# Attention over 746 tokens: queries and keys in parts of 512 and 234 instead of two parts of 373

## The chip, the cores and the metric

The kernel runs on one core of one Trainium2 chip. The metric is the device time of one execution in microseconds. The engines are named as the profile names them: PE (TensorE; PEld is its weight load), DVE (VectorE), ACT (ScalarE), POOL (GpSimd) and SP (SyncE, which issues most transfers).

## The reference, cut to what matters

The input holds 16 sequences of 750 frames with 23 features. A five-tap layer turns each into 746 tokens of 128 channels, with a batch norm over all of them. Then come an attention block with 8 heads of 16 channels and a feed-forward block in which a router picks one of 8 experts for each token.

```
h = tdnn(x)                                    # (16, 746, 128), relu, batch norm
z = layernorm(h)
q, k, v = heads(z @ Wq.T + bq), heads(z @ Wk.T + bk), heads(z @ Wv.T + bv)
scores = einsum('bhqd,bhkd->bhqk', q, k) / sqrt(16)
h = h + merge(softmax(scores) @ v) @ Wo.T + bo
z = layernorm(h); e = argmax(z @ Wr + br)
h = h + gate * (relu(z @ W1[e] + b1[e]) @ W2[e] + b2[e])
```

The softmax subtracts the maximum of each query over all 746 keys, so each head needs its scores twice: once to find the maxima, and once, transposed, for the exponentials.

## The kernel before, in words

The kernel is software-pipelined over the 16 sequences. A *body* (function `body(i, par)` of every engine) holds one turn of the pipeline, and there are 19 of them (i from -2 to 16). In a body the scores, exponentials and weighted sums of sequence i run, beside the maxima of sequence i and i+1, the layer norm and projections of sequence i+2, and the output projection, second layer norm and router of sequence i-1. Ahead of the bodies stands the five-tap layer, behind them the expert layer over 101 slots of 128 tokens.

A body has 96 steps, two times 48: heads 0 to 3 (g = 0), then heads 4 to 7 (g = 1). Within each half come two passes of 24 steps, one for each half of the queries (373 of 746). A step takes one head j and one tile of 128 keys (kt; the sixth has 106).

- **PE**, per step: a score quad (L1343; four matmuls of 32 weight columns, recorded at L1247 in `quad`) into one of three score banks, and a maximum quad (L1352) of 128 queries against 373 keys into one of three maximum banks. The maximum quads run `LEAD` = 60 steps ahead of the scores. At the steps of `WEIGH_AT` PE also issues `weigh` (L1312: four fp32 matmuls, exponentials against values), and at those of `FILLS` (L300) a smaller task: HTOK, PROJ, MAX1, XNT, Q, K, V, RANK, MAX0. All tasks of a steady body go through one bank (`misc`), so a task waits (`bank_free`) until the one before it has been read out.
- **ACT**, per step: the exponential of one score bank (L808), into a ring of three groups of four heads in SBUF (`probs`). At `OUT_AT` it copies the finished sum out (L817), and at `EMPTY_AT` it empties the tasks' bank.
- **DVE**, per step: the maximum over one maximum bank (L1112, `half_max`). Between these stand, each at the step that a table gives, the joining of the halves (`maxima`, L935 to L943), transposes and normalisation of the attention output (`T_AT`, `INV_AT`, `MULT_AT`, `BACK_AT`), the residual (`REST_AT`, L988 and L990, which empties PROJ), the layer-norm statistics (`LN1_AT`, `LN2_AT`), the router (`ROUTE_AT`) and the places of the tokens among the experts (`RANK_AT`, L1029 to L1046; its first instruction waits for the task RANK).
- **POOL** finishes the layer norms, splits q and k into bf16 parts and scatters rows; **SP** moves the q and k parts at the steps of `LOAD0_AT` and `LOAD1_AT`.

Every engine walks its own steps in order. What binds them are the rings: PE may write score bank s only when the exponential of step s-3 is done (L1342), and maximum bank m only when the reduction m-3 is done (L1351). So PE can be at most three steps ahead of ACT and of DVE, and a task's step number against the step at which another engine serves it says who has to wait.

Some numbers of the tables, before: RANK is issued at step 77 and DVE takes it up at 78; PROJ at 17 and 27, taken up at 24 and 38; MAX1 at 41, emptied at 42; MAX0 at 88.

Of the kernel before, what the change touches and what calls it, by code (L numbers as in the profile page):

```python
# [5 lines left out]
def audio_tower(  # L6
# [62 lines left out]
    STEPS = H * 2 * NT  # L69
    PASS = NT * GH  # L70
    GROUPS = STEPS // GH
    LEAD = 60


    PARTS = 1
    WEIGH_AT = (7, 11, 15, 19, 23, 27)
    OUT_AT = 4
    LN1_AT = (19, 21, 24, 25, 26, 28)
    LN2_AT = (40, 43, 45, 46, 48, 49)
    GATE_AT, H_AT = 73, (19, 26)  # L80
    T_AT, INV_AT, MULT_AT, BACK_AT, REST_AT = (55, 59, 6, 8), (66, 9), (85, 11), (12, 16), (24, 38)
    ROUTE_AT = (56, 57, 58, 60, 61, 63)
    RANK_AT = (78, 81, 82, 87, 89)
    LOAD1_AT = (26, 29, 32, 35, 38, 40, 46, 48, 50, 52, 54, 56)
    LOAD0_AT = (92, 94, 97, 99, 102, 104, 107, 109, 111, 114, 116, 118)
    SCATTER_AT = (0, 3, 6, 9, 12, 15)
# [12 lines left out]
    with ctx:  # L99
# [8 lines left out]
        RING, QW = N_P * GH * HALF, H * LP // 2  # L108
# [3 lines left out]
        probs = p_ring.rearrange("p (n j t) -> p n j t", n=N_P, j=GH)  # L112
        q_rows = [arena[0:KM, RING + QW * n:RING + QW * (n + 1)].bitcast(bf16).rearrange("p (h t) -> p h t", h=H)
# [15 lines left out]
        half_max = sb("half_max", [128, STEPS])  # L129
        neg_max = sb("neg_max", [128, STEPS // 2])  # L130
# [9 lines left out]
        mv2 = sb("mv2", [128, NT, 2])  # L140
        var_eps2 = sb("var_eps2", [128, NT])
        rstd2 = sb("rstd2", [128, NT])
        by_tok = sb("by_tok", [128, 2, LP])
        r_den = sb("r_den", [128, 2, LP // QUAD])
# [10 lines left out]
        place = sb("place", [128, NT, E])  # L155
        place1 = sb("place1", [128, NT, E])
# [4 lines left out]
        tok_w_sb = sb("tok_w_sb", [TAPS, D])  # L161
# [4 lines left out]
        bo_bc, br_bc, bv_sb = sb("bo_bc", [128, D]), sb("br_bc", [128, E]), sb("bv_sb", [128, 1])  # L166
        wo_wr = sb("wo_wr", [128, D + E])
        wr_c = sb("wr_c", [128, E])
        mean_w = sb("mean_w", [128, 128])
# [4 lines left out]
        bn_stats = sb("bn_stats", [128, 2 * B, 6])  # L174
# [30 lines left out]
        early_e, early_r, early_r0 = sb("early_e", [128, 1]), sb("early_r", [128, 1]), sb("early_r0", [128, 1])  # L205
        slot_e, slot_r, slot_r0 = sb("slot_e", [128, 1]), sb("slot_r", [128, 1]), sb("slot_r0", [128, 1])
        slot_e_i, slot_r_i = sb("slot_e_i", [1, 128], i32), sb("slot_r_i", [1, 128], i32)

        def of_ring(first, n):
# [93 lines left out]
        EMPTY_AT = {("HTOK", 0): 9, ("HTOK", 1): 14, ("MAX1", 0): 42, ("XNT", 0): 46, ("XNT", 1): 50,  # L303
                    ("Q", 0): (53, 54), ("Q", 1): (57, 58), ("K", 0): (61, 62), ("K", 1): (66, 70),
                    ("V", 0): 73, ("V", 1): 86, ("MAX0", 0): 88}
# [134 lines left out]
        def step_of(s):  # L440
            p, kt, j = s // PASS, s % PASS // GH, s % GH
            return p // 2, p % 2, kt, GH * (p // 2) + j, j
# [17 lines left out]
        def _(sp):  # L460
# [56 lines left out]
            def body(i, par):  # L517
# [27 lines left out]
                if live(i, 2):  # L545
                    if not is_body(i, FIRST_BODY):
                        store_q(i, (1, 2))
                        store_k(i, 1)
                        store_k(i, 2)
                    if live(i, 0):  # L550
                        sp.wait_ge(s_st, scores(i, STEPS // 2 - 1))
                    load_first_heads(i, par)
# [177 lines left out]
        def _(act):  # L730
# [67 lines left out]
            def body(i, par):  # L798
                if is_body(i, FIRST_BODY + 1):
                    constants()  # L800
                for s in range(STEPS):
                    if live(i, 0):
                        g, qh, kt, h, j = step_of(s)
                        G = s // GH
                        if j == 0:
                            wait(act, s_pv, i * GROUPS + (G - N_P + 1))
                        act.wait_ge(s_st, scores(i, s))
                        nc.scalar.activation(probs[0:kn(kt), G % N_P, j, :], st_bank[s % N_ST][0:kn(kt), 0:HALF],  # L808
                                             ACT.Exp).then_inc(s_exp, 1)
                    if s % PASS == OUT_AT:  # L810

                        b, p = (i, s // PASS - 1) if s >= PASS else (i - 1, 3)
                        if live(i, 0 if s >= PASS else -1):
# [3 lines left out]
                            nc.scalar.copy(o_un[:, p // 2, p % 2 * HALF:(p % 2 + 1) * HALF], o_bank[:, 0:HALF])\  # L817
                              .then_inc(s_o, 1)
# [54 lines left out]
        def _(dve):  # L873
# [55 lines left out]
            def maxima(b, g, n):  # L929

                k = 3 * g
                full = neg_max[:, 24 * g:24 * (g + 1)].rearrange("p (h t) -> p t h", h=GH)
                if n == 0:
                    dve.wait_ge(s_red, b * STEPS + STEPS // 2 * (g + 1))
                    nc.vector.tensor_reduce(neg_max[:, 24 * g:24 * (g + 1)],  # L935
                                            half_max[:, 48 * g:48 * (g + 1)].rearrange("p (n a) -> p n a", a=2),
                                            AX.X, ALU.max, negate=True).then_inc(s_max, 1)
                elif n == 1:
                    dve.wait_ge(s_max, b * 6 + (k + 1))
                    nc.vector.tensor_copy(max_parts[:, g, :, 0, :], full).then_inc(s_max, 1)  # L940
# [158 lines left out]
            def body(i, par):  # L1099
# [4 lines left out]
                for s in range(STEPS):  # L1104
# [5 lines left out]
                    if 0 <= b < B:  # L1110
                        dve.wait_ge(s_mx, b * STEPS + (m + 1))
                        nc.vector.tensor_reduce(half_max[:, m:m + 1], mx_bank[m % N_MX][:, 0:HALF], AX.X, ALU.max)\  # L1112
                          .then_inc(s_red, 1)
                    for g, at in ((1, STEPS - 1 - LEAD), (0, STEPS + STEPS // 2 - 1 - LEAD)):
# [20 lines left out]
                    if s == 33 and is_body(i, FIRST_BODY):  # L1135
# [11 lines left out]
                    if s == 72 and is_body(i, LAST_BODY):  # L1147
# [3 lines left out]
                    if s == 60 and is_body(i, FIRST_BODY):  # L1151
# [69 lines left out]
        def _(pe):  # L1221
# [77 lines left out]

            def weigh(b, G, k):  # L1300

                p, kt = G // NT, G % NT
                first = HALF * k // PARTS
                n = HALF * (k + 1) // PARTS - first
                if k == 0:
                    pe.wait_ge(s_exp, scores(b, GH * (G + 1) - 1))
                    if kt == 0:
                        wait(pe, s_o, b * 4 + p)  # L1310
                for j in range(GH):
                    last = nc.tensor.matmul(o_bank[32 * j:32 * (j + 1), first:first + n],  # L1312
                                            values[b % 3][0:kn(kt), kt, GH * (p // 2) + j, :],
                                            probs[0:kn(kt), G % N_P, j, first:first + n],
                                            start=kt == 0 and k == 0, stop=kt == NT - 1, skip_group_check=True)
                if k == PARTS - 1:
                    last.then_inc(s_pv, 1)
# [12 lines left out]
            def body(i, par):  # L1330
# [6 lines left out]
                for s in range(STEPS):  # L1337
                    if live(i, 0):
                        g, qh, kt, h, j = step_of(s)
                        if s % 48 == 0:  # L1340
                            pe.wait_ge(s_mrow, i * 64 + 32 * (g + 1))
                        wait(pe, s_exp, scores(i, s) - N_ST)  # L1342
                        quad(st_bank[s % N_ST][0:kn(kt), 0:HALF], k_rows[par][0:KM, h, D * kt:D * kt + kn(kt)],  # L1343
                             q_rows[par][0:KM, h, qh * HALF:(qh + 1) * HALF]).then_inc(s_st, 1)
                    b, m = maximum_of(i, s)
                    if 0 <= b < B:

                        h, t, half = m // 12, m % 12 // 2, m % 2
                        if m % 48 == 0:
                            pe.wait_ge(s_ld[m // 48], b * 192 + 192)  # L1350
                        wait(pe, s_red, b * STEPS + (m + 1 - N_MX))  # L1351
                        quad(mx_bank[m % N_MX][:, 0:HALF], q_rows[b % 2][0:KR, h, D * t:D * (t + 1)],  # L1352
                             k_rows[b % 2][0:KR, h, half * HALF:(half + 1) * HALF]).then_inc(s_mx, 1)
                    for n, after in enumerate(WEIGH_AT):

                        p = (s - after) // PASS
                        if (s - after) % PASS == 0 and live(i, 0 if p >= 0 else -1):
                            weigh(i if p >= 0 else i - 1, p % 4 * NT + n // PARTS, n % PARTS)
                    if is_body(i, LAST_BODY) and s == WEIGH_AT[-1] - PASS + 1:
# [87 lines left out]
```

## Time and profile before

| | |
|---|---|
| time, median of 3 runs | 1233.38 us (1231.71 to 1234.83) |
| span of the profiled execution | 1275.9 us |
| PE busy | 1178.7 us, 92% of the span |
| DVE busy | 1072.5 us, 84% |
| ACT busy | 950.6 us, 75% |
| POOL busy | 680.0 us, 53% |
| chain that ended last, by engine | PE 63%, DVE 20%, issue 5%, POOL 3%, ACT 2% |
| L1112, DVE reductions of 373 | 1536, 760.8 us busy, mean 534 ns |
| L808, ACT exponentials of 373 | 1536, 655.0 us busy, mean 489 ns |
| L1247, score and maximum quads | 2 x 6144 matmuls of 373 columns, 515.7 and 519.1 us busy |
| L1312, weighing, fp32 | 3072 records, 313.2 us busy |

The profile gives no time of the profiled execution besides its span. That span is 42.5 us above the median of the timed runs. Matmuls overlap, so the durations of a line of PE are longer than what each adds; the distance from one start to the next is the better measure, and the same holds for DVE and ACT when they run back to back.

### The profile page before, as it was taken

The numbers are of one execution on the slowest core, as the hardware profiler recorded it, in microseconds if no ns is written. First come the engines' busy times: TensorE is split into PE (matmuls) and PEld (weight loads), VectorE is DVE, ScalarE is ACT, GpSimd is POOL, SyncE is SP. The second block draws the span as 40 slices with busy tenths as digits, with TensorE's granted clock in tenths as the row PEclk, the third lists the DMA queues.
The fourth block names the chain that finished last, engine by engine and source line by source line (L and its number), as shares of the span: only waits on it lengthen the run. The fifth ranks groups of instructions, "written<-read, shape, count | busy, mean of one in ns | idle before, by whom it ended". The sixth has DMA issues, their size and how long they took to land.

```text
span 1275.9 us, 53879 instructions
## 1 busy us (share of the span) xinstructions
PE 1178.7 (92%) x21379; PEld 745.5 (58%) x21379; DVE 1072.5 (84%) x2756; ACT 950.6 (75%) x2477; POOL 680.0 (53%) x894
## 2 busy tenths in 40 slices
PE   6479999999999999999999999999999846899996
PEld 3334656555555556555555556565644326899996
DVE  7469899999999999999999999999999544577774
ACT  4426988888887878788888878797877824567774
POOL 2062436566473837475665739374723334456664
PEclk9768999999999999999999999999999969899998
DMA  8152132222313131323223131313220513333331
GB/s 190 39 84 79 40 86 72 76 84 61 94 52 94 45 105 42 104 72 79 83 63 93 51 94 45 106 41 104 72 80 28 150 56 105 88 93 105 103 101 50
DMA packets 79409, 102.32 MB, mean 80 GB/s; under 512 B 15916, under 2 KB 72995, under 8 KB 78734
## 3 DMA queue, kind: packets, MB, share of 16 engines
q1 hardware_dynamic: 70624, 79.02, 23.4%
q0 software_dynamic: 8384, 20.22, 5.1%
q8 instruction: 158, 2.59, 0.9%
q14 instruction: 57, 0.47, 0.1%
q10 hardware_dynamic: 186, 0.02, 0.0%
HBM read 60.76 MB, written 38.93 MB: 78 GB/s over the span
## 4 chain that ended last, share of the span: by engine, by line
PE 63%; DVE 20%; issue 5%; POOL 3%; ACT 2%; DMA 1%; SPq 1%; another core or an unknown queue 1%; POOLq 0%; DVEq 0%; ACTq 0%
PE psum L1247 36%; DVE half_max L1112 14%; PE psum L1312 13%; PE psum L1391 6%; PE psum L1401 5%; PE psum L1252 2%; ACT arena L808 2%; DVE stats L916 1%; POOL out_dram L720 1%; DVE rows L990 1%; PE psum L1382 1%; POOL arena L405 1%; DMA arena<-max_rows 1%; PE psum L1267 1%; DVE arena L962 1%
## 5 line engine op out<-in xcount | busy, mean ns | idle before, releaser
L1112 DVE TENSOR_REDUCE half_max<-psum 128x1 f32<-128x373 f32 x1536 | 760.8, 534 | 62.8 <-PE psum L1247 55.0
L808 ACT ACTIVATE arena<-psum 128x373 f32<-128x373 f32 (+1 forms) x1536 | 655.0, 489 | 154.4 <-PE psum L1247 139.0
L1247 PE MATMUL psum<-k_rows,arena 96*32 96x373 bf16 x6144 | 519.1, 329 | 14.9 <-DVE half_max L1112 6.1
L1247 PE MATMUL psum<-arena,k_rows 98*32 98x373 bf16 x6144 | 515.7, 326 | 13.7 <-ACT arena L808 6.2
L1312 PE MATMUL psum<-arena,values 128*32 128x373 f32 (+1 forms) x3072 | 313.2, 478 | 0.2
L1247 PEld LDWEIGHTS psum<-k_rows,arena 96*32 96x32 bf16 x6144 | 173.8, 96 | 195.7 <-DVE half_max L1112 103.4
L1247 PEld LDWEIGHTS psum<-arena,k_rows 98*32 98x32 bf16 x6144 | 176.4, 95 | 178.2 <-ACT arena L808 74.8
L631 POOL DMA_INDIRECT routed_rows_dram<-rows,pos_i x96 | 96.6, 1007 | 170.7 <-PE psum L1247 106.2
L720 POOL DMA_INDIRECT out_dram<-arena,slot_id x101 | 119.2, 1180 | 90.0 <-issue 51.5
L1312 PEld LDWEIGHTS psum<-arena,values 128*32 128x32 f32 (+1 forms) x3072 | 98.4, 110 | 20.7 <-issue 2.8
L861 ACT COPY arena<-psum 128x128 f32<-128x128 f32 x101 | 26.9, 266 | 77.7 <-PE psum L1382 39.7
L639 POOL TENSOR_TENSOR m_diff<-stats 128x6 f32<-128x6 f32 x15 | 3.1, 203 | 147.1 <-DVE stats L916 147.1
L1391 PE MATMUL psum<-arena,seq 128*128 128x128 f32 x544 | 75.3, 283 | 5.1 <-issue 2.4
L852 ACT ACTIVATE arena<-psum,seq 128x128 f32<-128x128 f32 x272 | 77.8, 370 | 0.5 <-issue 0.5
L1401 PE MATMUL psum<-seq,arena 128*128 128x128 f32 x544 | 73.8, 280 | 0.3 <-ACT arena L852 0.3
L1391 PEld LDWEIGHTS psum<-arena,seq 128*128 128x128 f32 x544 | 69.1, 199 | 6.5 <-issue 5.0
L405 POOL TENSOR_SCALAR arena<-h_cur,m_mean,rstd 128x128 f32<-128x128 f32 x90 | 70.9, 800 | 3.3 <-POOL rstd L665 3.3
L405 POOL TENSOR_SCALAR rows<-rows,n_mean,rstd 128x128 f32<-128x128 f32 x90 | 70.8, 796 | 0.0
L1401 PEld LDWEIGHTS psum<-seq,arena 128*128 128x128 f32 x544 | 67.6, 195 | 0.5 <-ACT arena L852 0.5
L1097 DVE COPY seq<-seq 128x1156 f32 x68 | 53.6, 788 | 11.1 <-issue 1.4
L950 DVE STREAM_TRANSPOSE by_tok<-o_un 128x384 f32<-128x384 f32 x64 | 36.2, 566 | 18.7 <-ACT o_un L817 18.7
L1209 DVE TENSOR_TENSOR arena<-psum,seq 128x128 f32<-128x128 f32 x68 | 19.8, 291 | 35.3 <-PE psum L1401 30.9
(218 smaller groups left out, 1447.5 us busy)
## 6 DMA issues: line engine op xcount, KB each, us to landing
arena<-q_parts_dram SPq DMA_DIRECT2D x192, 93.2 KB, 2.4
k_rows<-k_parts_dram SPq DMA_DIRECT2D x192, 93.2 KB, 2.4
arena<-routed_rows_dram SPq DMA_DIRECT2D x101, 130.0 KB
q_parts_dram<-q_part SPq DMA_DIRECT2D x48, 186.5 KB, 2.3
k_parts_dram<-k_part SPq DMA_DIRECT2D x48, 186.5 KB, 2.0
arena<-in_x_t_dram SPq DMA_DIRECT2D x3, 703.1 KB, 14.1
seq<-in_w_dram SPq DMA_DIRECT2D x1, 2048.0 KB
seq<-in_w_dram SPq DMA_DIRECT2D x8, 256.0 KB
```

What stands on the lines that cost most here:

```text
L405: last = ops.tensor_scalar(dst(t), src(t), mean_var[:, t, 0:1], r_root[:, t:t + 1], ALU.subtract, ALU.mult)
L631: pool.indirect_dma_start(out=rows_dram, out_offset=bass.IndirectOffsetOnAxis(ap=pos_i[:, t:t + 1], axis=0), in_=rows[:, t, :], in_offset= ...
L720: pool.indirect_dma_start(out=out_rows, out_offset=bass.IndirectOffsetOnAxis(ap=slot_id[:, n:n + 1], axis=0), in_=slot_y[n][:, :], in_offs ...
L808: nc.scalar.activation(probs[0:kn(kt), G % N_P, j, :], st_bank[s % N_ST][0:kn(kt), 0:HALF], ACT.Exp).then_inc(s_exp, 1)
L852: last = nc.scalar.activation(slot_ht[n % 2][:, D * k:D * (k + 1)], psum[:, 2 + n % 2, D * k:D * (k + 1)], ACT.Relu, bias=slot_w[n % N_W][ ...
L950: nc.vector.transpose(by_tok[:, g, first:first + LP // 2], o_un[:, g, first:first + LP // 2])\
L1097: nc.vector.tensor_copy(slot_w[n % N_W].unsqueeze(1), w_sb[:, bass.ds(e, 1), :]).then_inc(s_fw, 1)
L1112: nc.vector.tensor_reduce(half_max[:, m:m + 1], mx_bank[m % N_MX][:, 0:HALF], AX.X, ALU.max)\
L1247: last = nc.tensor.matmul(dst[n:n + m], weights[:, n:n + m], moving, start=start, stop=stop)
L1312: last = nc.tensor.matmul(o_bank[32 * j:32 * (j + 1), first:first + n], values[b % 3][0:kn(kt), kt, GH * (p // 2) + j, :], probs[0:kn(kt), ...
L1391: last = nc.tensor.matmul(psum[:, 2 + n % 2, D * k:D * (k + 1)], slot_w[n % N_W][:, W1 + D * k:W1 + D * (k + 1)], slot_xt[n % 2][:, :], st ...
L1401: last = nc.tensor.matmul(psum[:, 5 + n % 3, 0:D], slot_ht[n % 2][:, D * k:D * (k + 1)], slot_w[n % N_W][:, W2 + D * k:W2 + D * (k + 1)], ...
```

## The change: what it does

Each head's 746 queries (for the scores) and 746 keys (for the maxima) are cut at 512. The 512 fill one PSUM bank alone (a *wide* step); the 234 of two heads share one bank (a *narrow* step, 468 columns, two quads on PE, one instruction on ACT or DVE). A body then has 72 steps, two halves of 36. For the scores, 24 wide steps come first in each half, then 12 narrow ones. For the maxima, each run of three steps is wide, wide, narrow.

- PE issues as many quads as before (96 of 512 columns and 96 of 234 in place of 192 of 373). `weigh` runs in 6 wide and 6 narrow groups a half, at new steps.
- The ring of exponentials is larger (three groups of 4 x 512), and the narrow exponentials use the same memory in six pieces, so ACT waits on other `weigh` groups (`weighed_before`).
- The output copy is of 512 and then of 234 columns; `turn` waits for the copy that its half needs.
- All step tables are rewritten for 72 steps. RANK is now issued at step 61, and DVE takes it up at step 58. PROJ is issued at 13 and 21 and taken up at 18 and 28. MAX1 is issued at 29. V's second part comes after RANK and MAX0. `LEAD` is 48.
- Some small tiles share memory with others (`place` with `scored`, `mv2` with `mv`, tables and constants in `by_tok`).

```
-    STEPS = H * 2 * NT
-    LEAD = 60
-    WEIGH_AT = (7, 11, 15, 19, 23, 27)
-    OUT_AT = 4
-    LN1_AT = (19, 21, 24, 25, 26, 28)
-    T_AT, INV_AT, MULT_AT, BACK_AT, REST_AT = (55, 59, 6, 8), (66, 9), (85, 11), (12, 16), (24, 38)
-    RANK_AT = (78, 81, 82, 87, 89)
+    WIDE_Q = 512
+    NARROW_Q = L - WIDE_Q
+    WIDE_STEPS = NT * GH
+    HALF_STEPS = WIDE_STEPS + NT * GH // 2
+    STEPS = 2 * HALF_STEPS
+    LEAD = 48
+    WEIGH_AT = (7, 11, 15, 19, 23, 27, 31, 32, 34, 35, 37, 39)
+    OUT_AT = (28, 40)
+    LN1_AT = (14, 15, 17, 18, 19, 21)
+    T_AT, INV_AT, MULT_AT, BACK_AT, REST_AT = (41, 44, 5, 6), (50, 7), (64, 8), (9, 12), (18, 28)
+    RANK_AT = (58, 60, 61, 65, 67)
...
-        FILLS = (("HTOK", 0, 9), ("HTOK", 1, 13), ("PROJ", 0, 17), ("PROJ", 1, 27), ("MAX1", 0, 41), ("XNT", 0, 46),
-                 ("XNT", 1, 49), ("Q", 0, 53), ("Q", 1, 57), ("K", 0, 61), ("K", 1, 65), ("V", 0, 73),
-                 ("RANK", 0, 77), ("V", 1, 85), ("MAX0", 0, 88))
+        FILLS = (("HTOK", 0, 5), ("HTOK", 1, 9), ("PROJ", 0, 13), ("PROJ", 1, 21), ("MAX1", 0, 29), ("XNT", 0, 33),
+                 ("XNT", 1, 36), ("Q", 0, 41), ("Q", 1, 45), ("K", 0, 49), ("K", 1, 53), ("V", 0, 57),
+                 ("RANK", 0, 61), ("MAX0", 0, 65), ("V", 1, 69))
...
+                        if wide:
+                            nc.scalar.activation(probs[0:kn(kt), kt % N_P, j, :], st_bank[s % N_ST][0:kn(kt), 0:WIDE_Q],
+                                                 ACT.Exp).then_inc(s_exp, 1)
+                        else:
+                            nc.scalar.activation(narrow_probs[0:kn(kt), kt, NARROW_Q * j:NARROW_Q * (j + 2)],
+                                                 st_bank[s % N_ST][0:kn(kt), 0:2 * NARROW_Q],
+                                                 ACT.Exp).then_inc(s_exp, 1)
...
+                        n, part = m // 3, m % 3
+                        if part < 2:
+                            nc.vector.tensor_reduce(half_max[:, n, part:part + 1], mx_bank[m % N_MX][:, 0:WIDE_Q], AX.X, ALU.max)\
+                              .then_inc(s_red, 1)
+                        else:
+                            nc.vector.tensor_reduce(half_max[:, n, 2:4],
+                                                    mx_bank[m % N_MX][:, 0:2 * NARROW_Q].rearrange("p (a t) -> p a t", a=2),
+                                                    AX.X, ALU.max).then_inc(s_red, 1)
...
+                            for n in range(2):
+                                last = quad(st_bank[s % N_ST][0:kn(kt), NARROW_Q * n:NARROW_Q * (n + 1)],
+                                            k_rows[par][0:KM, h + n, D * kt:D * kt + kn(kt)], q_rows[par][0:KM, h + n, WIDE_Q:L])
+                            last.then_inc(s_st, 1)
```

## Rows read from the trace of the kernel before

**Rows 1.** The page: the span, and the engines' busy time

```profile
span 1275.9 us, 53879 instructions
...
PE 1178.7 (92%) x21379; PEld 745.5 (58%) x21379; DVE 1072.5 (84%) x2756; ACT 950.6 (75%) x2477; POOL 680.0 (53%) x894
```

**Rows 2.** Stretches: one steady body, then RANK's end to MAX1, MAX1 to RANK's end

```profile
core 0: us, PE busy (x) PEld busy (x) DVE busy (x) ACT busy (x) POOL busy (x), PEclk, DMA share, GB/s
561.08:619.65 58.57, 57.76 (x1228) 33.21 (x1224) 54.85 (x140) 49.24 (x123) 35.91 (x51) 1.00 0.28 76
558.18:594.24 36.06, 35.25 (x752) 18.85 (x737) 34.04 (x88) 28.73 (x73) 16.02 (x22) 1.00 0.34 91
594.24:616.76 22.52, 22.52 (x493) 14.34 (x493) 20.82 (x53) 20.53 (x51) 19.90 (x30) 1.00 0.18 51
```

**Rows 3.** Timeline of DVE: the joining of the maxima (start us, us, engine, line)

```profile
210.56 0.20 DVE L935 TENSOR_REDUCE neg_max<-half_max 128x24 f32<-128x48 f32 x1
...
913.84 0.20 DVE L935 TENSOR_REDUCE neg_max<-half_max 128x24 f32<-128x48 f32 x1
```

**Rows 4.** The chain that ended last, in order of time: start us, us, what

```profile
561.53 0.35 DVE place L1039
...
563.67 0.47 DVE arena L962
...
587.29 0.20 DVE stats L916
...
588.59 3.17 DVE half_max L1112 x7
...
591.79 0.20 DVE neg_max L935
...
592.44 0.18 DVE max_parts L940
...
593.07 0.10 DVE max_parts L943
...
593.63 0.09 DVE raw L988
593.72 0.47 DVE rows L990
...
594.24 0.39 PE psum L1267 x4
...
957.33 0.48 DVE by_tok L950
```

**Rows 5.** Timeline of PE and PEld: weighing, score and maximum quads, RANK

```profile
600.15 0.11 PEld L1247 LDWEIGHTS psum<-k_rows,arena 96*32 96x32 bf16 x4
...
610.69 0.83 PE L1312 MATMUL psum<-arena,values 128*32 128x373 f32 x8
611.32 0.37 PE L1247 MATMUL psum<-arena,k_rows 98*32 98x373 bf16 x4
611.48 0.37 PE L1247 MATMUL psum<-k_rows,arena 96*32 96x373 bf16 x4
...
616.51 0.20 PE L1247 MATMUL psum<-onehot,before 128*32 128x56 bf16 x4
616.54 0.30 PE L1247 MATMUL psum<-onehot,ones_b 128*32 128x48 bf16 x24
616.70 0.24 PE L1247 MATMUL psum<-zero_b,ones_b 128*32 128x56 bf16 x4
616.76 0.35 PE L1247 MATMUL psum<-arena,k_rows 98*32 98x373 bf16 x4
```

**Rows 6.** Timeline of DVE: a reduction of 48 elements and the next start

```profile
955.53 0.20 DVE L1002 TENSOR_REDUCE top<-logits 128x6 f32<-128x48 f32 x1 [0.46 <-POOL logits L695]
955.65 0.54 DVE L1112 TENSOR_REDUCE half_max<-psum 128x1 f32<-128x373 f32 x1
```

**Rows 7.** Timeline of ACT: exponentials back to back, after the last maximum

```profile
1012.70 1.60 ACT L808 ACTIVATE arena<-psum 128x373 f32<-128x373 f32 x4 [0.18 <-PE psum L1247]
...
1014.48 1.60 ACT L808 ACTIVATE arena<-psum 106x373 f32<-106x373 f32 x4 [0.18 <-PE psum L1247]
```

More of the change, by code:

```diff
@@ L154, in audio_tower @@
         g_inv = sb("g_inv", [128, NT])
-        place = sb("place", [128, NT, E])
-        place1 = sb("place1", [128, NT, E])
+        place, place1 = scored, scored2
         pos = sb("pos", [128, NT])
@@ L204, in audio_tower @@
         late_base, late_first = sb("late_base", [128, 1]), sb("late_first", [128, 1])
-        early_e, early_r, early_r0 = sb("early_e", [128, 1]), sb("early_r", [128, 1]), sb("early_r0", [128, 1])
-        slot_e, slot_r, slot_r0 = sb("slot_e", [128, 1]), sb("slot_r", [128, 1]), sb("slot_r0", [128, 1])
-        slot_e_i, slot_r_i = sb("slot_e_i", [1, 128], i32), sb("slot_r_i", [1, 128], i32)
+        slot_cols = sb("slot_cols", [128, 6])
+        early_e, early_r, early_r0, slot_e, slot_r, slot_r0 = (slot_cols[:, n:n + 1] for n in range(6))
+        slot_e_i, slot_r_i = (by_tok[0:1, 0, D * n:D * (n + 1)].bitcast(i32) for n in range(2))
         def of_ring(first, n):
@@ L440, in step_of, with last_step_of, weighed_before @@
         def step_of(s):
-            p, kt, j = s // PASS, s % PASS // GH, s % GH
-            return p // 2, p % 2, kt, GH * (p // 2) + j, j
+            g, r = s // HALF_STEPS, s % HALF_STEPS
+            if r < WIDE_STEPS:
+                return g, True, r // GH, r % GH
+            return g, False, (r - WIDE_STEPS) // 2, (r - WIDE_STEPS) % 2 * 2
+        def last_step_of(G):
+            g, n = G // HALF_GROUPS, G % HALF_GROUPS
+            return HALF_STEPS * g + (GH * n + GH - 1 if n < NT else WIDE_STEPS + 2 * (n - NT) + 1)
+        def weighed_before(i, g, wide, kt):
+            first = i * GROUPS + g * HALF_GROUPS
+            if not wide:
+                return first + NT // 2 + kt // 2 + 1
+            return first + kt - 2 if kt >= N_P else first - NT + 2 * kt + 2
         def load_patches(engine, c, low, high):
@@ L550, in body @@
                     if live(i, 0):
-                        sp.wait_ge(s_st, scores(i, STEPS // 2 - 1))
+                        sp.wait_ge(s_st, scores(i, HALF_STEPS - 1))
                     load_first_heads(i, par)
@@ L802, in body @@
                     if live(i, 0):
-                        g, qh, kt, h, j = step_of(s)
-                        G = s // GH
+                        g, wide, kt, j = step_of(s)
                         if j == 0:
-                            wait(act, s_pv, i * GROUPS + (G - N_P + 1))
+                            wait(act, s_pv, weighed_before(i, g, wide, kt))
                         act.wait_ge(s_st, scores(i, s))
[L808 to L813, printed above, removed]
+                        if wide:
[5 more added lines that the diff above has]
+                                                 ACT.Exp).then_inc(s_exp, 1)
+                    for p, at in ((0, OUT_AT[0]), (1, OUT_AT[1]), (2, HALF_STEPS + OUT_AT[0]), (3, OUT_AT[1] - HALF_STEPS)):
+                        b, ahead = (i, 0) if p < 3 else (i - 1, -1)
+                        if s == at and live(i, ahead):
                             act.wait_ge(s_pv, b * GROUPS + NT * (p + 1))
@@ L931, in maxima @@
                 k = 3 * g
-                full = neg_max[:, 24 * g:24 * (g + 1)].rearrange("p (h t) -> p t h", h=GH)
+                n_g = GH * NT
+                full = neg_max[:, n_g * g:n_g * (g + 1)].rearrange("p (u t a) -> p t u a", u=2, a=2)
+                high, low = (max_parts[:, g, :, part, :].rearrange("p t (u a) -> p t u a", a=2) for part in range(2))
                 if n == 0:
-                    dve.wait_ge(s_red, b * STEPS + STEPS // 2 * (g + 1))
-                    nc.vector.tensor_reduce(neg_max[:, 24 * g:24 * (g + 1)],
-                                            half_max[:, 48 * g:48 * (g + 1)].rearrange("p (n a) -> p n a", a=2),
+                    dve.wait_ge(s_red, b * STEPS + HALF_STEPS * (g + 1))
+                    nc.vector.tensor_reduce(neg_max[:, n_g * g:n_g * (g + 1)].rearrange("p (n a) -> p n a", a=2),
+                                            half_max[:, n_g // 2 * g:n_g // 2 * (g + 1), :].rearrange("p n (c a) -> p n a c", c=2),
                                             AX.X, ALU.max, negate=True).then_inc(s_max, 1)
@@ L1134, in body @@
                             layer_moments(stats, mv, var_eps, s_ln, 0)
-                    if s == 33 and is_body(i, FIRST_BODY):
+                    if s == 24 and is_body(i, FIRST_BODY):
                         dve.wait_ge(s_ln_p, 1)
@@ L1146, in body @@
                             layer_moments(stats2, mv2, var_eps2, s_ln2, B - 1)
-                    if s == 72 and is_body(i, LAST_BODY):
+                    if s == 54 and is_body(i, LAST_BODY):
                         dve.wait_ge(s_ln2_p, ln2_p_done(B - 1) + 3)
@@ L1150, in body @@
                                   mv2, rstd2, s_ln2_p)
-                    if s == 60 and is_body(i, FIRST_BODY):
+                    if s == 55 and is_body(i, FIRST_BODY):
                         split(dve, nc.vector, s_apart_v, i, "Q")
@@ L1298, in task, with weigh @@
                 last.then_inc(s_misc, 1)
[L1300 to L1310, printed above, removed]
-                for j in range(GH):
[L1312 to L1317, printed above, removed]
+            def weigh(b, G):
+                g, n = G // HALF_GROUPS, G % HALF_GROUPS
+                wide, kt = n < NT, n % NT
+                pe.wait_ge(s_exp, scores(b, last_step_of(G)))
+                if kt == 0:
+                    wait(pe, s_o, b * 4 + G // NT)
+                for j in range(GH):
+                    if wide:
+                        moving = probs[0:kn(kt), kt % N_P, j, :]
+                    else:
+                        moving = narrow_probs[0:kn(kt), kt, NARROW_Q * j:NARROW_Q * (j + 1)]
+                    last = nc.tensor.matmul(o_bank[32 * j:32 * (j + 1), 0:WIDE_Q if wide else NARROW_Q],
+                                            values[b % 3][0:kn(kt), kt, GH * g + j, :], moving,
+                                            start=kt == 0, stop=kt == NT - 1, skip_group_check=True)
+                last.then_inc(s_pv, 1)
             def constants():
@@ L1345, in body @@
                     b, m = maximum_of(i, s)
                     if 0 <= b < B:
-                        h, t, half = m // 12, m % 12 // 2, m % 2
-                        if m % 48 == 0:
-                            pe.wait_ge(s_ld[m // 48], b * 192 + 192)
+                        u, t, n = m // (3 * NT), m % (3 * NT) // 3, m % 3
+                        if m % HALF_STEPS == 0:
+                            pe.wait_ge(s_ld[m // HALF_STEPS], b * 192 + 192)
                         wait(pe, s_red, b * STEPS + (m + 1 - N_MX))
-                        quad(mx_bank[m % N_MX][:, 0:HALF], q_rows[b % 2][0:KR, h, D * t:D * (t + 1)],
-                             k_rows[b % 2][0:KR, h, half * HALF:(half + 1) * HALF]).then_inc(s_mx, 1)
@@ L1354, in body @@
-                    for n, after in enumerate(WEIGH_AT):
[L1356 to L1359, printed above, removed]
+                        if n < 2:
+                            quad(mx_bank[m % N_MX][:, 0:WIDE_Q], q_rows[b % 2][0:KR, 2 * u + n, D * t:D * (t + 1)],
+                                 k_rows[b % 2][0:KR, 2 * u + n, 0:WIDE_Q]).then_inc(s_mx, 1)
+                        else:
+                            for a in range(2):
+                                last = quad(mx_bank[m % N_MX][:, NARROW_Q * a:NARROW_Q * (a + 1)],
+                                            q_rows[b % 2][0:KR, 2 * u + a, D * t:D * (t + 1)],
+                                            k_rows[b % 2][0:KR, 2 * u + a, WIDE_Q:L])
+                            last.then_inc(s_mx, 1)
@@ L1360, in body @@
+                    for n, after in enumerate(WEIGH_AT):
+                        for g in (0, 1):
+                            at = HALF_STEPS * g + after
+                            if at % STEPS == s and live(i, -(at // STEPS)):
+                                weigh(i - at // STEPS, HALF_GROUPS * g + n)
+                    if is_body(i, LAST_BODY) and s == WEIGH_AT[-1] - HALF_STEPS + 1:
                         pe.wait_ge(s_early, EARLIES)
```

65 lines of the change are left out of this document (32 added, 33 removed).

## The prediction

> **What bounds the kernel now.** I read the page first: PE is busy for 92% of the span and DVE for 84% [rows 1], so neither is plainly the bound. Next come the stretches of one steady body. The joining of the first maxima comes back twelve times between 210.56 and 913.84 us [rows 3], 58.6 us apart on average, and the body cut out for closer reading takes 58.57 us at a granted clock of 1.00 [rows 2]. Sixteen such bodies make some 940 of the 1275.9 us. Last, the chain in order of time shows that the bound changes inside a body. From MAX1 to RANK the chain is PE's alone, and PE is busy for 22.52 of 22.52 us [rows 2]. From RANK round to the next MAX1, 36.06 us, the chain jumps between runs of DVE reductions (seven in 3.17 us), the small DVE work between them, and PE [rows 4]. I call the first the PE stretch and the second the DVE stretch.
>
> The DVE stretch by counts: DVE passes steps 78 to 95 and 0 to 38, 57 reductions of 3.17 / 7 = 0.453 us [rows 4], 25.8 us. Between them stand, by [rows 4], two joinings of maxima (0.20 + 0.18 + 0.10 each, 0.96), two normalisations (0.47 each, 0.94), four transposes (0.48 each, 1.92), six statistics (0.20, 1.2), two residuals (0.09 + 0.47, 1.1), the ranks (0.35 and four small ones at 0.12 [rows 6], 0.8) and a reciprocal (0.2): 7.1. Together 32.9, so 3.2 of the 36.06 us are neither: DVE waited for a bank that PE had not yet filled, or for a semaphore.
>
> PE in the same stretch: 60 steps of two quads at 0.160 us (611.32 to 611.48) make 19.2, and 15 weighings at 0.63 (610.69 to 611.32) 9.5 [rows 5]: 28.7 plus tasks. In the PE stretch it is 36 steps (11.5) and 9 weighings (5.7), 17.2, so tasks and rests take 22.52 - 17.2 = 5.3. The tasks of the DVE stretch are of the same kind and I put them at no more than that.
>
> **The change part by part.**
>
> *PE's work: nothing.* A score or maximum quad takes 0.160 us at 373 columns. Six quads of RANK, 28 columns on average, take 0.16 together (616.54 to 616.70), 0.027 each [rows 5]. The line between them gives 0.214 at 512 and 0.106 at 234. A pair costs 0.320 either way, and there are 96 pairs before and after. Weighing in proportion to columns: 0.865 wide and 0.395 narrow, the sum of two unchanged. Bounds for a narrow quad: 0.100 (pure proportion) to 0.160 (no cheaper than now, if its weight loads, 0.11 us for four [rows 5], came to the surface). I take 0.106, since RANK's quads load just as many weights and pass at 0.027.
>
> *DVE's reductions: 1.7 us less a body.* A reduction of 48 elements lets the next start after 0.12 us [rows 6], one of 373 after 0.453: 1.025 ns an element. That makes 0.595 at 512 and 0.550 at 468, 0.580 on average. 96 x 0.453 = 43.5 becomes 48 x 0.595 + 24 x 0.550 = 41.8. Bounds: 0 (pure proportion) to 2.9 (24 instructions at the 0.12 of the shortest). In the DVE stretch alone it is 42 x 0.580 = 24.4 for 25.8, 1.4 less.
>
> The Trainium skill, "VectorE: DVE Perf Modes", section on the TRN2 errata, gives an operation that reads PSUM a fixed 120 cycles, 125 ns at 0.96 GHz, beside one cycle an element. By it a reduction of 373 would take 0.513, and the DVE stretch would lose about 2.3 us in place of 1.4 (an estimate from that page), some 14 us over sixteen bodies. The trace has 0.453 from start to start, so I stay with the row.
>
> *ACT's exponentials: nothing on the path.* Four in a row take 1.60 us, and in the tail the next four start 1.78 us after the first [rows 7]. The columns of a body are the same (96 x 373), so ACT's work at worst stays as it is, and at best it falls by as much per instruction as DVE's does. ACT is busy for 49.24 of 58.57 us [rows 2] and keeps that slack.
>
> *The rings in time: longer.* Three banks are still three steps, but a step lasts 58.57 / 72 = 0.81 us for 0.61, so that DVE's small work of 0.2 to 0.5 us is covered better. This is the gain that I can't count, only bound: between none and all of the 3.2 us.
>
> *Two meetings: new waits.* RANK goes out on PE at step 61, and DVE takes it up at 58, where before it was 77 and 78. DVE must stand at step 58, with reductions 59, 60 and 61 queued behind it, until PE has done steps 59 to 61 and the task. PE can do that much (maximum 61 needs reduction 58 alone), so there is no deadlock, but PE then stands before maximum 62 until DVE has taken up RANK and done reduction 59. At the other end MAX1 (PE step 29) needs the bank that DVE empties at the end of its step 28; before it was 41 against 38. So PE may not be three steps ahead there, but must wait for DVE. Between the meetings nothing can be carried over from one stretch into the other: a body is the DVE chain from RANK to MAX1, and then PE's work from MAX1 to RANK.
>
> What the trace of before shows of such a stand: `top` sat 0.46 us for POOL, and the reduction behind it started 0.12 us after it, not before [rows 6]. The Trainium skill says so too ("PSUM — Partial Sum Buffer", Engine vs sequencer instructions: the queue of VectorE is strict FIFO). If the reductions could pass, the stand would cost DVE nothing, about 0.4 us a body less, and 1220 in place of the forecast; by this rule they can't.
>
> *The sum of a body.* DVE stretch: DVE now passes steps 59 to 71 and 0 to 28, 42 reductions, 24.4, and the same 7.1: 31.5. PE there: 40 steps of two quads at 0.213 (17.0), 7 wide and 6 narrow weighings (6.1 + 2.4), 25.5, plus at most 5.3: 30.8. So DVE sets it. To this I add 1.0 us for rests: 0.4 at the meeting (from RANK's last quad to reduction 59), and about 0.1 a step in steps 71 to 4, where no small work stands on DVE (five reductions 2.9) and PE needs as long (five steps 2.1 and two narrow weighings 0.8). Before those, DVE starts three full banks behind, and from step 5 on it carries transposes, normalisation and statistics, so it can't run dry. 32.5. PE stretch: 22.52, with 32 steps (13.6) and 5 wide and 6 narrow weighings (4.3 + 2.4) in place of 17.2: 25.6. Together 58.1 for 58.57, 0.5 us less, 8 us over sixteen bodies.
>
> *Both ends.* `LEAD` is two thirds of a body where it was five eighths: before the first scores DVE needs 48 x 0.580 = 27.8 for 60 x 0.453 = 27.2, 0.6 more. After the last maximum the same share of scores runs alone, with a fifth fewer exponentials; I take nothing for it, bounds -2 to +1. Shared tiles, later loads and the fewer steps of SP and POOL I put at nothing: POOL is busy for 35.91 of 58.57 us [rows 2]. If that cover were gone, a wait of DVE for POOL like the 0.46 of [rows 6] would come once a body, 7 us.
>
> In all 7.4 us less: 1268.5 for the span of 1275.9. The span is 42.5 us above the median of the timed runs, and I know no reason why the bodies should be what differs, so I take the same 7.4 from 1233.4: 1226.
>
> **The rivals.**
>
> - *The meetings eat more than the longer rings give: slower.* Place: DVE's stand at step 58 and PE's at MAX1. If the DVE stretch keeps all of its 3.2 us of rests, the body is 31.5 + 3.2 + 25.6 = 60.3, 28 us slower in all, 1261; half way, 1245. It decides as soon as the rests exceed 58.57 - 57.1 = 1.5 us. For it: those 3.2 us came about with a freer coupling than the new one. Against it: the reductions behind the stand have their banks full. 25%.
> - *No rests at all:* DVE is never short between the meetings, 31.5 + 25.6 = 57.1 or a little less, 24 to 28 us gained, 1207. For it: longer rings. Against it: every semaphore hop. 12%.
> - *It comes out even:* rests of 1.3 to 1.7, 1230 to 1237. 17%.
> - *The change doesn't do what it says, because narrow quads are no cheaper:* 96 x (0.160 - 0.106) = 5.2 us a body, 1316. RANK's row speaks against it. 3%.
>
> **How the numbers follow.** A measurement of this kernel can tell about 0.3%, 3.7 us, from no change. The forecast (rests 0.4 to 1.3; 1217 to 1230) holds 43%, and with the case of no rests faster gets 55%. Even gets 17%, and the two slower cases 28%. The range leaves out the lower half of the no-rests case, the upper part of the slower rival and the last: 1206 to 1252.
>
> **What would show it.** In the profile after, reductions of 512 and 468 should start 0.595 and 0.550 apart, narrow quads 0.106. The body should be 58.1 us. DVE should have one idle piece before `place` (L1029 before), released by PE's RANK, of 0.5 to 2 us in every body, and PE an idle piece before MAX1, released by DVE's `rows`. From MAX1 to RANK PE should be busy throughout for 25.6 us. The prediction is wrong if a narrow quad costs more than 0.12, if the DVE stretch is above 33.5 us, or if another wait (POOL's logits, a q or k load) shows up once a body.

## The result and the profile after

The changed kernel takes 1247.06 us (median of 4 runs, 1246.54 to 1248.33) against 1233.55 for the kernel before. The ratio is 1.0105, with a 95% interval of 1.009 to 1.0121: 13.5 us slower, where 7.4 us faster was forecast.

A span of a steady body is best taken from the joining of the maxima. These are the first and the last of thirteen such rows, twelve bodies apart, from DVE's timeline of the changed kernel (start us, us, engine, line).

```profile
206.79 0.20 DVE L957 TENSOR_REDUCE neg_max<-half_max 128x24 f32<-128x48 f32 x1
...
904.77 0.20 DVE L957 TENSOR_REDUCE neg_max<-half_max 128x24 f32<-128x48 f32 x1
```

That is 58.17 us a body (twelve bodies in 697.98 us), where 58.1 was forecast. The page's span, and the stretches of the prediction, in the changed kernel: one body, RANK's end to MAX1, MAX1 to RANK's end (columns as in [rows 2]).

```profile
span 1244.7 us, 53111 instructions
```

```profile
core 0: us, PE busy (x) PEld busy (x) DVE busy (x) ACT busy (x) POOL busy (x), PEclk, DMA share, GB/s
556.06:614.17 58.11, 55.78 (x1224) 32.97 (x1224) 53.35 (x115) 47.89 (x97) 35.98 (x51) 1.00 0.27 76
555.02:587.37 32.35, 30.35 (x693) 17.64 (x679) 31.75 (x71) 25.52 (x52) 13.98 (x21) 1.00 0.35 99
587.37:613.10 25.73, 25.40 (x547) 15.29 (x548) 21.61 (x45) 22.33 (x47) 21.97 (x31) 1.00 0.16 47
```

The two stretches are 32.35 and 25.73 us; forecast were 32.5 and 25.6. Against [rows 2] the first is 3.7 shorter, the second 3.2 longer. By the two profiles the change should have made the kernel faster, and indeed its span, 1244.7, is 31 us below the 1275.9 of [rows 1]. But the timed runs of the kernel before take 1233.5. So the profile of before may not be typical, and the first experiment takes it again.

### The profile page after: what moved, and what is told of

Same layout as the page of the kernel before. It is cut to its first block, busy times and chain, and to the rows that moved or that the text cites. A ratio compares the mean times of both kernels' runs of the same rounds, so it can differ in the third digit from the quotient of the medians.

```text
span 1244.7 us, 53111 instructions
## 1 busy us (share of the span) xinstructions
PE 1138.9 (92%) x21379; PEld 741.4 (60%) x21379; DVE 1048.7 (84%) x2372; ACT 926.6 (74%) x2093; POOL 679.9 (55%) x894
## 4 chain that ended last, share of the span: by engine, by line
PE 56%; DVE 23%; POOL 10%; issue 4%; ACT 1%; DMA 1%; SPq 1%; POOLq 0%; DVEq 0%; ACTq 0%
PE psum L1274 28%; PE psum L1339 11%; DVE half_max L1135 11%; PE psum L1431 7%; PE psum L1441 7%; POOL arena L407 6%; DVE half_max L1138 5%; DVE stats L936 2%; POOL rstd L682 2%; PE psum L1279 1%; DVE by_tok L971 1%; DVE merged_t L992 1%; PE psum L1422 1%; DVE arena L983 1%; ACT arena L825 1%
## 5 line engine op out<-in xcount | busy, mean ns | idle before, releaser
L1135 DVE TENSOR_REDUCE half_max<-psum 128x1 f32<-128x512 f32 x768 | 508.1, 678 | 35.3 <-PE psum L1274 32.7
L1274 PE MATMUL psum<-k_rows,arena 96*32 96x512 bf16 (+1 forms) x6144 | 462.0, 326 | 24.4 <-DVE half_max L1138 10.5
L825 ACT ACTIVATE arena<-psum 128x512 f32<-128x512 f32 (+1 forms) x768 | 428.2, 600 | 66.5 <-PE psum L1274 60.2
L1274 PE MATMUL psum<-arena,k_rows 98*32 98x512 bf16 (+1 forms) x6144 | 458.2, 322 | 2.8 <-ACT arena L825 1.4
L1339 PE MATMUL psum<-arena,values 128*32 128x234 f32 (+3 forms) x3072 | 313.9, 476 | 0.8 <-ACT arena L828 0.4
L1138 DVE TENSOR_REDUCE half_max<-psum 128x2 f32<-128x468 f32 x384 | 243.1, 633 | 8.3 <-PE psum L1274 7.0
L828 ACT ACTIVATE arena<-psum 128x468 f32<-128x468 f32 (+1 forms) x384 | 198.0, 557 | 66.3 <-PE psum L1274 64.0
```

Source lines behind the costliest of these rows:

```text
L825: nc.scalar.activation(probs[0:kn(kt), kt % N_P, j, :], st_bank[s % N_ST][0:kn(kt), 0:WIDE_Q], ACT.Exp).then_inc(s_exp, 1)
L828: nc.scalar.activation(narrow_probs[0:kn(kt), kt, NARROW_Q * j:NARROW_Q * (j + 2)], st_bank[s % N_ST][0:kn(kt), 0:2 * NARROW_Q], ACT.Exp). ...
L1135: nc.vector.tensor_reduce(half_max[:, n, part:part + 1], mx_bank[m % N_MX][:, 0:WIDE_Q], AX.X, ALU.max)\
L1138: nc.vector.tensor_reduce(half_max[:, n, 2:4], mx_bank[m % N_MX][:, 0:2 * NARROW_Q].rearrange("p (a t) -> p a t", a=2), AX.X, ALU.max).the ...
L1274: last = nc.tensor.matmul(dst[n:n + m], weights[:, n:n + m], moving, start=start, stop=stop)
L1339: last = nc.tensor.matmul(o_bank[32 * j:32 * (j + 1), 0:WIDE_Q if wide else NARROW_Q], values[b % 3][0:kn(kt), kt, GH * g + j, :], moving, ...
```

## The experiments

### The kernel before, profiled once more (e1)

No edit.

> The kernel before, unchanged, profiled once more. The profile that the prediction was read from has a span of 1275.9 us, 42 above the timed median, while the changed kernel's profile (1244.7) agrees with its timed runs. Theory A (that profile was of an untypical execution, and its steady body of 58.57 us was too long): the span is now 1230 to 1236 and the steady body 56 to 57 us, so that the changed kernel's 58.1 is 1 to 2 us a body worse. Theory B (the bodies were typical and only front and tail were stretched): the span is 1230 to 1236 but the steady body is again 58.5 us and the 42 us lie ahead of the first and behind the last joining of maxima (97.6 and 277 us in that profile; 94.3 and 259.5 in the changed kernel's). Then the changed kernel would lose in front and tail, not in the bodies.

The span is now 1232.6 us, in line with the timed runs. From the page, DVE's timeline (again first and last of thirteen) and the stretches of this run of the kernel before:

```profile
span 1232.6 us, 53879 instructions
```

```profile
209.42 0.20 DVE L935 TENSOR_REDUCE neg_max<-half_max 128x24 f32<-128x48 f32 x1
...
889.80 0.20 DVE L935 TENSOR_REDUCE neg_max<-half_max 128x24 f32<-128x48 f32 x1
```

```profile
core 0: us, PE busy (x) PEld busy (x) DVE busy (x) ACT busy (x) POOL busy (x), PEclk, DMA share, GB/s
549.93:606.58 56.65, 56.49 (x1232) 33.56 (x1228) 54.61 (x140) 49.09 (x122) 35.86 (x51) 1.00 0.28 78
545.76:579.91 34.15, 34.00 (x755) 19.20 (x736) 33.83 (x88) 28.59 (x73) 15.97 (x22) 1.00 0.35 96
579.91:602.43 22.52, 22.52 (x493) 14.36 (x493) 20.79 (x53) 20.52 (x51) 19.91 (x30) 1.00 0.18 51
```

A body is 56.70 us and not 58.6 ([rows 3]). Theory A holds: the profile that the prediction was read from had bodies that were 1.9 us too long, all of it in the stretch from RANK to MAX1 (36.06 for 34.15), while the other stretch is the same to the hundredth (22.52). Its granted clock was 1.00 in both. Why that one execution was slower is not settled: counted step by step, the two traces part between steps 94 and 23, where in the slower one DVE and ACT take up their banks up to 1.2 us later behind PE's recorded quads than in the other, and they agree everywhere else.

So the change costs 58.17 - 56.70 = 1.47 us a steady body, 17.6 us in twelve. Some of it comes back outside these twelve bodies: the first joining of maxima stands at 94.30 (95.86 before), the time behind the last is 259.5 us (261.5), and the bodies just ahead of and behind the twelve are 2.0 us shorter together. That leaves the 12.1 us between the spans 1244.7 and 1232.6.

### The three waits, one by one and together (e2 to e5)

The changed kernel has three places in every body where PE waits; for a body of the retaken profile of before the same view lists none. All rows are of the changed kernel. PE's waits in one body (us in total, times, longest):

```profile
PE psum L1294 <- DVE rows L1011: 1.0, 1, 1.0
PE psum L1274 <- DVE half_max L1138: 0.7, 1, 0.7
PE psum L1279 <- POOL arena L407: 0.3, 1, 0.3
PE psum L1274 <- DVE half_max L1135: 0.2, 1, 0.2
```

The second and the fourth belong to RANK, the first to MAX1, the third to XNT. By the rows below they sum to some 2.3 us.

RANK. DVE's and PE's timeline around the take-up of RANK (the name `scored` is `place` before):

```profile
552.84 0.38 PE L1274 MATMUL psum<-k_rows,arena 96*32 96x234 bf16 x8
...
554.93 0.25 PE L1274 MATMUL psum<-zero_b,ones_b 128*32 128x56 bf16 x4
...
555.27 0.21 DVE L1050 TENSOR_TENSOR scored<-psum,next_row 128x48 f32<-128x48 f32 x1 [1.72 <-PE psum L1274]
555.40 0.63 DVE L1138 TENSOR_REDUCE half_max<-psum 128x2 f32<-128x468 f32 x1
556.06 0.20 DVE L957 TENSOR_REDUCE neg_max<-half_max 128x24 f32<-128x48 f32 x1
556.08 0.38 PE L1274 MATMUL psum<-k_rows,arena 96*32 96x234 bf16 x8 [0.69 <-DVE half_max L1138]
556.92 0.40 PE L1274 MATMUL psum<-k_rows,arena 96*32 96x512 bf16 x4 [0.25 <-DVE half_max L1135]
```

DVE stands 1.72 us, up to 555.27. The bank of reduction 59 is filled by the quads of 552.84, before the stand begins, and those of 60 and 61 fill during it, but no reduction passes the standing instruction. Then PE stands 0.69 us for reduction 59 and 0.25 for the next. The Trainium skill ("PSUM — Partial Sum Buffer", Engine vs sequencer instructions) has VectorE's queue as a strict FIFO, and the row agrees.

MAX1. PE's row:

```profile
587.37 0.39 PE L1294 MATMUL psum<-identb,max_parts 128*8 128x128 bf16 x4 [0.99 <-DVE rows L1011]
```

PE waits 0.99 us for the second residual, which stands only one step ahead of MAX1.

XNT. POOL's timeline from the statistics to the normalised rows, and PE's row for the task that waits for them:

```profile
582.35 0.20 POOL L656 TENSOR_TENSOR m_diff<-stats 128x6 f32<-128x6 f32 x1 [8.06 <-DVE stats L936]
...
584.24 1.36 POOL L682 TENSOR_TENSOR rstd<-var_eps,minus_half 128x6 f32<-128x6 f32 x1
585.81 4.71 POOL L407 TENSOR_SCALAR arena<-h_cur,m_mean,rstd 128x128 f32<-128x128 f32 x6 [0.22 <-POOL rstd L682]
```

```profile
589.95 0.38 PE L1274 MATMUL psum<-k_rows,arena 96*32 96x512 bf16 x1
590.67 0.52 PE L1279 MATMUL psum<-ident,arena 128*128 128x128 f32 x3 [0.33 <-POOL arena L407]
```

POOL idles 8.06 us for the last statistics of DVE and then needs 8.2 us, from 582.35 to 590.52. From start to start PE loses 0.5 us to it: 0.72 from its last wide quad to XNT, less the 0.22 that such a quad takes. The row's own 0.33 counts from that quad's modelled end. Before, the last statistics stood at step 28 and XNT at 46, 18 steps of 0.59 us (10.6); now they stand at 21 and 33, 12 steps of 0.81 (9.7). The table was scaled and POOL's 8.2 us were not, and how far DVE is behind PE has to fit in as well.

The edits, each on the changed kernel; e5 has all three:

```
# e2, RANK taken up behind its issue
-    RANK_AT = (58, 60, 61, 65, 67)
+    RANK_AT = (62, 63, 64, 66, 67)
-                 ("RANK", 0, 61), ("MAX0", 0, 65), ("V", 1, 69))
+                 ("RANK", 0, 61), ("MAX0", 0, 66), ("V", 1, 69))
# e3, second residual three steps ahead of MAX1
-    ... (9, 12), (18, 28)
+    ... (9, 12), (18, 26)
# e4, XNT two steps later
-    ("XNT", 0, 33), ("XNT", 1, 36)
+    ("XNT", 0, 35), ("XNT", 1, 38)
```

(`...` marks what is left out of a line; `EMPTY_AT` follows for MAX0 and XNT. e2 moves MAX0 by a step as well, and no run takes that apart.)

> The changed kernel with one wait undone: DVE takes up RANK at steps 62 to 67 instead of 58 to 67 (PE issues it at 61 as before), and MAX0 moves from 65 to 66. In the changed kernel PE has idle pieces of 0.89 and 0.42 us behind RANK in every body. Theory A (the three new waits, RANK's stand, MAX1's and XNT's, each cost what PE's idle pieces show): 1 us a body, 1231 to 1236 for 1247. Theory B (the DVE chain binds from RANK to MAX1 whatever PE waits for there): DVE only gets ahead, PE then waits at MAX1 or XNT instead, 1243 to 1248. Theory C (the larger steps themselves cost): 1243 or more, and all three undone together stay above 1240.

> The changed kernel with one wait undone: the second residual, which empties the bank that MAX1 needs, stands at DVE step 26 instead of 28, so three steps ahead of MAX1 (29) as it was before. PE idles 1.16 us before MAX1 in every body of the changed kernel. Theory A: 0.8 us a body, 1233 to 1237. Theory B: POOL's layer norm, whose last statistics stay at step 21, holds XNT at step 33 now for longer by what PE gained, 1243 to 1248. Theory C: 1243 or more.

> The changed kernel with one wait undone: XNT is issued at PE steps 35 and 38 instead of 33 and 36. In the changed kernel XNT waits 0.67 us in every body for POOL's layer norm, which follows the statistics at DVE step 21 by 8.3 us. Theory A: 0.67 us a body, 1235 to 1238. Theory B: the same, since this wait lies in the PE stretch: 1235 to 1238. Theory C: 1243 or more.

> The three edits together (RANK taken up at 62, second residual at 26, XNT at 35 and 38). Theory A: 1.0 + 0.8 + 0.67 us a body, some 35 to 40 us in all, 1207 to 1215, below the kernel before (1233.5). Theory B: the stretch from RANK to MAX1 is again bound by DVE's chain of 31.5 us and the rest by PE's 25.1: a body of 56.6 to 57.2, 1222 to 1232. Theory C: above 1240.

| kernel | us | ratio to before, 95% | steady body |
|---|---|---|---|
| changed | 1247.1 | 1.0105 (1.009 to 1.0121) | 58.17 |
| e2, RANK | 1236.5 | 1.0012 (1.0000 to 1.0024) | 57.37 |
| e3, residual | 1247.2 | 1.0098 (1.0071 to 1.0125) | 58.13 |
| e4, XNT | 1238.9 | 1.0033 (1.0016 to 1.0049) | 57.62 |
| e5, all three | 1216.6 | 0.9850 (0.9825 to 0.9874) | 56.02 |

The ratios are to the kernel before, timed again beside each group of runs: its median is 1233.55 us beside the changed kernel, 1235.41 beside e2 to e5 and 1234.76 beside e6 to e9. Differences in microseconds across groups are therefore good to 1 or 2 us.

Theory C is out: with the waits gone the larger steps are 1.5% faster than the kernel before. Theory A is right for RANK and XNT, though each gains a little less than its range has: 10.6 and 8.1 us, or 11.5 and 8.9 by the ratios. For the residual it is wrong and B is right: alone it gains nothing. The stretches of e3 and PE's timeline show where it went. The first stretch is 31.20 us, 1.15 shorter, and the second 26.87, longer by the same, since XNT still waits for POOL, now 1.27 us:

```profile
555.65:586.85 31.20, 30.19 (x697) 17.69 (x681) 30.59 (x69) 24.36 (x50) 12.82 (x20) 1.00 0.36 102
586.85:613.72 26.87, 25.60 (x555) 14.89 (x548) 22.57 (x47) 23.22 (x49) 23.11 (x32) 1.00 0.16 46
```

```profile
591.30 0.52 PE L1279 MATMUL psum<-ident,arena 128*128 128x128 f32 x3 [1.27 <-POOL arena L407]
```

For e5 neither A (1207 to 1215) nor B (1222 to 1232) has the number; it lies next to A. Its stretches (one body, RANK's end to MAX1, MAX1 to RANK's end):

```profile
594.80:650.84 56.04, 55.80 (x1255) 32.86 (x1237) 53.80 (x116) 47.67 (x99) 36.00 (x51) 1.00 0.28 79
594.80:625.25 30.45, 30.21 (x710) 17.99 (x692) 30.14 (x67) 24.40 (x51) 12.64 (x20) 1.00 0.37 105
625.25:650.84 25.59, 25.59 (x557) 14.87 (x545) 23.66 (x50) 23.27 (x49) 23.36 (x32) 1.00 0.17 49
```

In all of this body the profile shows no wait of PE for another engine, and the body is 2.15 us shorter than the changed kernel's, close to the 2.3 us of its waits. From MAX1 to RANK PE is busy throughout, as it was before the change. The DVE stretch is 30.45, below the 31.5 that I had as the least: with RANK taken up at 62, DVE no longer stands when RANK ends, but has done reduction 59 and is in 60.

### Two of three, and the other way round (e6 to e9)

e6 is e5 without the residual's edit, e7 is e5 without RANK's. e8 is the kernel *before* with one number changed, e9 is e5 with the first normalisation moved.

```
# e8, on the kernel before
-    RANK_AT = (78, 81, 82, 87, 89)
+    RANK_AT = (74, 81, 82, 87, 89)
# e9, on e5
-    T_AT, INV_AT, MULT_AT, ... (50, 7), (64, 8)
+    T_AT, INV_AT, MULT_AT, ... (50, 7), (52, 8)
```

> The changed kernel with RANK taken up at 62 and XNT at 35 and 38, but the second residual left at step 28, one step ahead of MAX1. Alone, the three edits gave -10.6 (RANK), 0 (residual) and -8.1 us (XNT), together -30.4. Theory A (the residual matters only once the others are gone, because the POOL chain to XNT starts from statistics that a late PE doesn't delay): the two together give 10.6 + 8.1 = 19, 1228, and the residual's share of the 30.4 is 11 to 12 us. Theory B (RANK and XNT alone make the gain, more than additive, and the residual is without effect): 1216 to 1220.

> The changed kernel with the second residual at 26 and XNT at 35 and 38, but RANK still taken up at 58, three steps before PE issues it. Theory A (the stand at RANK costs by itself, some 0.7 to 0.9 us a body whatever the rest does): 1228 to 1232. Theory B (the stand costs only what the other two waits make of it): 1216 to 1221.

> The kernel before with the stand of the changed one put in: DVE takes up RANK at step 74 where PE issues it at 77 (78 before). Nothing else is changed. Theory A (a take-up ahead of the issue forces PE to stop until DVE has served the task and one reduction): 0.6 to 1.0 us a body, 1243 to 1250 for 1234. Theory B (with the kernel before's shorter steps and DVE's slack from MAX1 to RANK it is absorbed): 1232 to 1237.

> The three edits together, and the first normalisation (0.47 us on DVE) moved from DVE step 64 to 52, so out of the stretch from RANK to MAX1, where DVE's chain is long, into the one where PE is busy throughout. Theory A (DVE's work from RANK to MAX1 lies on the path, moved work is gained in full): 0.47 us a body, 1209 to 1210 for 1216.6. Theory B (with the waits gone PE's own work bounds the body, 54.2 of 55.9 us): 1214 to 1217.

| kernel | us | ratio to before, 95% | what it tells |
|---|---|---|---|
| e6, RANK and XNT | 1229.6 | 0.9956 (0.9941 to 0.9972) | the residual is worth 12.9 us once the others are gone |
| e7, residual and XNT | 1225.6 | 0.9922 (0.9902 to 0.9943) | RANK's stand costs 9.0 us |
| e8, before with the stand | 1246.4 | 1.0090 (1.0061 to 1.0119) | the same stand costs the kernel before 11.7 us |
| e9, all and normalisation | 1213.8 | 0.9823 (0.9801 to 0.9846) | 2.8 us more |

e6 is near theory A: the residual gains 12.9 us behind the other two and nothing alone, since POOL's start is given by the statistics of step 21 and not by PE. e7 lies below A's range and above B's. The stand costs by itself, but 0.65 us a body (56.68 for 56.02) and not A's 0.7 to 0.9. e8 is the clearest. DVE's timeline of it, in a kernel that is otherwise the one before, and its stretches:

```profile
606.69 0.55 DVE L1112 TENSOR_REDUCE half_max<-psum 128x1 f32<-128x373 f32 x1 [0.30 <-PE psum L1247]
608.58 0.21 DVE L1029 TENSOR_TENSOR place<-psum,next_row 128x48 f32<-128x48 f32 x1 [1.34 <-PE psum L1247]
608.70 2.35 DVE L1112 TENSOR_REDUCE half_max<-psum 128x1 f32<-128x373 f32 x5
```

```profile
550.83:585.78 34.95, 34.19 (x763) 19.10 (x744) 34.39 (x89) 28.73 (x73) 16.00 (x22) 1.00 0.32 94
585.78:608.30 22.52, 22.52 (x492) 14.33 (x492) 20.02 (x51) 20.53 (x51) 19.91 (x30) 1.00 0.18 51
```

The stand is 1.34 us on DVE, right behind a wait of 0.30 us for PE, so DVE has slack there, and still the body grows from 56.70 to 57.45. All of it lies from RANK to MAX1 (34.95 for 34.15); the other stretch stays at 22.52. What DVE misses in the stand it owes in the stretch behind. e9 falls between the theories: of 0.47 us moved out of the DVE stretch 0.25 are gained a body (55.77 for 56.02), so DVE's work binds that stretch only in part. What binds the rest is not shown.

## Why the prediction was wrong, point by point

- **The base, wrong, and it turned the sign.** The prediction said of the 42.5 us between span and median: "I know no reason why the bodies should be what differs, so I take the same 7.4". The bodies were what differed. Retaken they last 56.70 us, and 58.1 against 56.70 over sixteen bodies would have given some 22 us slower. Outside the twelve steady bodies 5.5 us come back, 3.6 of them in front and tail. With the base went the gain: of the 3.2 us of rests in the DVE stretch, which the longer rings were to shorten, the retaken profile leaves 34.15 - 32.9, some 1.3. The rival "the meetings eat more than the longer rings give" had 25%; its point of decision (rests above 1.5 us) was reckoned from the same 58.57. With 56.70 it lies below zero: 57.1 without any rests is above it already. So the rival's time came (1247) and not its way, for the body is as long as forecast. Its "half way, 1245" isn't the sum of its terms either: with half of the 3.2 us, 31.5 + 1.6 + 25.6 is 58.7, some 1236.
- **PE's work and DVE's reductions, right.** Two narrow quads of the changed kernel take 0.20 us (554.33 to 554.53 in PE's timeline, the first fence below), where 0.106 each was forecast; the 0.160 that weight loads at the surface would have given is out. A narrow reduction lasts 0.55 from start to start (584.93 to 585.48 in DVE's, the second fence), two wide ones 1.20; forecast were 0.550 and 0.595 each.

```profile
554.33 0.38 PE L1274 MATMUL psum<-arena,k_rows 98*32 98x234 bf16 x8
554.53 0.40 PE L1274 MATMUL psum<-k_rows,arena 96*32 96x512 bf16 x4
```

```profile
584.93 0.64 DVE L1138 TENSOR_REDUCE half_max<-psum 128x2 f32<-128x468 f32 x1
585.48 1.28 DVE L1135 TENSOR_REDUCE half_max<-psum 128x1 f32<-128x512 f32 x2
586.68 0.17 DVE L1009 TENSOR_TENSOR raw<-psum,h_wr 128x24 f32<-128x24 f32 x1
```

  By the rule weighed in the prediction (the Trainium skill, "VectorE: DVE Perf Modes", the section on the TRN2 errata: 120 cycles beside the columns) a wide one would take 0.66 (an estimate from that page); the trace has 0.60.
- **The meetings, right in place, and cheap only against the wrong base.** The stand at RANK was forecast at 0.5 to 2 us on DVE and is 1.72, and PE's wait ahead of MAX1 is there. I had put rests of 1.0 us on the first stretch, 32.5, and it is 32.35. What I did not do is price both meetings against a kernel without them. The 0.4 us a body put on RANK's is too small: the stand costs 0.65 by e7 and 0.75 by e8. All three waits cost 2.15 us a body by e5, 30 us in all.
- **POOL at nothing, wrong.** I had read POOL's 35.91 busy of 58.57 us as cover, and named another of its waits (the logits) as the risk. The chain from LN1's last statistics to XNT is what the smaller step numbers uncovered: 8.1 us by e4. It is another wait once a body, which the prediction named as a sign of being wrong. The second stretch, 25.73 us for 25.6, has XNT's wait in it; with XNT moved it lasts 25.34 (e4, the row below) or 25.59 (e5). So PE's work there was put up to 0.3 too high, and the wait that was left out filled that: luck, in part.

```profile
582.04:607.38 25.34, 25.34 (x548) 16.17 (x549) 21.55 (x45) 22.36 (x47) 22.17 (x31) 1.00 0.16 47
```

- **Both ends: 0.6 more forecast, 3.6 less found.** No run takes this apart.
- **The larger steps, a gain once the waits are gone; the longer rings as its cause, not shown.** By the spans of e5 and e1 the gain is 17.5 us: 8.1 in the twelve bodies (56.02 for 56.70), 7.0 in the bodies around them, 2.3 ahead of the first joining, next to nothing in the tail. DVE's reductions, some 1.5 us less a body by the starts above (24 x 1.75 for 96 x 0.453), may explain it as well as longer rings do, and no run tells the two apart.

## What to carry to other kernels

Before a profile's durations are subtracted from anything, hold its span against the timed runs: a span 3.4% above the median is not a detail of front and tail until the repeating part is shown to be the same. When a table of step numbers is scaled, list for every consumer how many steps it stands behind its producer: a distance that went from 1 to -3, and one that went from 3 to 1, each came out as a new wait here, and a distance that covers a chain in microseconds must be scaled in microseconds. A single edit that takes away a visible wait of 1 us gained nothing here while the next wait stood right behind it; try the edits together too.

## What the runs showed that I had not expected

One execution of an unchanged kernel had every steady body 1.9 us longer (58.6 for 56.7) in the same steps, body after body, at a granted clock of 1.00, and none of the other executions profiled here shows it. Its cause stays open.
